# Perceiver layer: which engine normalises the rows of the later context chunks

## The reference

```python
def layer_norm(x, g, b):
    mu = jnp.mean(x, axis=-1, keepdims=True)
    var = jnp.mean((x - mu) ** 2, axis=-1, keepdims=True)
    return (x - mu) * jax.lax.rsqrt(var + EPS) * g + b

xn = layer_norm(x, g1, b1)            # context, (2, 2048, 512)
ln_lat = layer_norm(latents, g2, b2)
q = ln_lat @ Wq
kv = jnp.concatenate([xn, ln_lat], axis=1) @ Wkv
k, v = jnp.split(kv, 2, axis=-1)      # 16 heads of 64
weight = jnp.einsum('bhld,bhnd->bhln', q * scale, k * scale)
weight = softmax(where(full_mask, weight, neg))
out = jnp.einsum('bhln,bhnd->bhld', weight, v) @ Wout
```

## Time and profile before

| | us |
|---|---|
| median of 3 runs | 868.83 (868.0 to 869.57) |
| profiled execution | 869.66 |
| its span, first to last instruction | 867.9 |
| PE busy | 840.7 (97%) |
| DVE busy | 576.1 (66%) |
| ACT busy | 441.0 (51%) |
| POOL busy | 349.9 (40%) |

### The profile page before, as it was taken

One profiled execution on the slowest core, in us unless ns is written; L12 is line 12 of the kernel. 1 busy time (PEld: TensorE's weight loads), 2 busy tenths in 40 slices (PEclk: granted clock), 3 DMA queues, 4 the chain that ended last, 5 costly groups with the idle time before them and its releaser, 6 DMA issues.

```text
span 867.9 us, 17399 instructions
## 1 busy us (share of the span) xinstructions
PE 840.7 (97%) x6329; PEld 782.9 (90%) x6329; DVE 576.1 (66%) x1536; ACT 441.0 (51%) x1029; POOL 349.9 (40%) x361
## 2 busy tenths in 40 slices
PE   5999999999999999999999999999999999998998
PEld 3999999999999999999999999998977689986886
DVE  7454647566576878656576665777777547766886
ACT  5665454554556464644645545455435434344553
POOL 5742634534463655746454344313301310003443
PEclk9999999999999999999999999999999999999999
DMA  6554427576467757576675664787577676842310
GB/s 215 183 176 164 151 104 238 192 233 226 176 224 256 255 207 280 203 232 201 223 242 205 235 207 163 264 342 256 195 250 298 292 303 273 358 141 102 98 50 25
DMA packets 71126, 183.04 MB, mean 211 GB/s; under 512 B 6353, under 2 KB 19585, under 8 KB 65025
## 3 DMA queue, kind: packets, MB, share of 16 engines
q1 hardware_dynamic: 70944, 181.90, 59.0%
q10 hardware_dynamic: 96, 0.02, 0.0%
HBM read 130.00 MB, written 50.86 MB: 208 GB/s over the span
## 4 chain that ended last, share of the span: by engine, by line
PE 85%; DVE 7%; DMA 4%; issue 2%; ACT 2%; SPq 0%; POOL 0%; DVEq 0%; ACTq 0%
PE pJ L1660 15%; PE pJ L1661 14%; PE pJ L1662 14%; PE pV L1806 7%; PE pS L1784 4%; PE pT L1792 3%; PE pS L1792 3%; PE pS L1660 2%; PE pT L1784 2%; PE pS L1662 2%; PE pS L1661 2%; DMA w_split<-wvst 2%; PE pX L1696 1%; PE pV L1660 1%; PE pV L1661 1%
## 5 line engine op out<-in xcount | busy, mean ns | idle before, releaser
L1660 PE MATMUL pJ<-WV,XT 128*128 128x256 f32 x544 | 158.5, 291 | 0.0
L1661 PE MATMUL pJ<-WV,XT 128*128 128x256 f32 x544 | 153.8, 283 | 0.0
L1662 PE MATMUL pJ<-WV,XT 128*128 128x256 f32 x544 | 153.7, 283 | 0.0
L862 ACT ACTIVATE SP<-SP,xneg 128x768 f32<-128x768 f32 (+1 forms) x96 | 85.8, 895 | 119.3 <-DVE xneg L1235 119.3
L1660 PE MATMUL pJ<-XT,WK 128*128 128x384 f32 (+1 forms) x384 | 126.9, 330 | 3.6 <-DVE XT L1135 1.4
L1662 PE MATMUL pJ<-XT,WK 128*128 128x384 f32 (+1 forms) x384 | 125.2, 326 | 0.0
L1661 PE MATMUL pJ<-XT,WK 128*128 128x384 f32 (+1 forms) x384 | 125.1, 326 | 0.0
L1135 DVE TENSOR_TENSOR KT<-pJ,KT 128x384 fp32r<-128x384 f32 x96 | 51.2, 535 | 89.8 <-ACT KT L839 89.3
L1660 PEld LDWEIGHTS pJ<-WV,XT 128*128 128x128 f32 x544 | 104.1, 191 | 0.2 <-issue 0.2
L1661 PEld LDWEIGHTS pJ<-WV,XT 128*128 128x128 f32 x544 | 104.2, 192 | 0.0
L1662 PEld LDWEIGHTS pJ<-WV,XT 128*128 128x128 f32 x544 | 104.0, 191 | 0.0
(11 more groups left out here) (397 smaller groups left out, 2153.8 us busy)
## 6 DMA issues: line engine op xcount, KB each, us to landing
WS<-w_split SPq DMA_DIRECT2D x14, 2048.0 KB, 8.8
WV<-wv_split SPq DMA_DIRECT2D x20, 1024.0 KB, 7.2
WK<-wk_split SPq DMA_DIRECT2D x40, 512.0 KB, 4.5
w_split<-wkst SPq DMA_DIRECT2D x40, 512.0 KB, 3.6
w_split<-wvst SPq DMA_DIRECT2D x40, 512.0 KB, 3.9
XA<-w_split SPq DMA_DIRECT2D x4, 2048.0 KB, 13.0
xraw<-in_ctx SPq DMA_DIRECT2D x7, 768.0 KB, 6.4
wk_split<-WK SPq DMA_DIRECT2D x8, 512.0 KB, 4.0
```

The lines of the kernel that those rows point to most:

```text
L862: ac.activation(SP[:, I % 2, h, 0:w], SP[:, I % 2, h, 0:w], ACT.Exp, bias=xneg[:, I % 2, h:h + 1], scale=XSC, accum_out=total).then_inc(c_ ...
L1660: te.matmul(dst, a(HI), b(HI), start=start, stop=False)
L1661: te.matmul(dst, a(HI), b(LO), start=False, stop=False)
L1662: return te.matmul(dst, a(LO), b(HI), start=False, stop=stop)
```

## The change

For chunks 3 to 11 (nine chunks, 24 tiles) the rows are normalised by ScalarE. GpSimd computes `nmr = -mean * rstd` behind `rstd` with two small instructions, and ScalarE then applies `rstd * x + nmr` to each tile in place. These instructions stand in ScalarE's list in iterations 3, 7, ... 35, behind the exponentials and `rescale` of the next iteration and ahead of the copy of `V{G}.2`.

```diff
+            def negative_means(C):
+
+                m = ctx_count(C)
+                pool.wait_ge(c_rstd, C + 1)
+                pool.wait_ge(c_norm, C - 2)
+                gp.tensor_tensor(nmr[:, 0:m], mv[:, 0:m, 0], rstd[:, 0:m], ALU.mult).then_inc(s_rst, 1)
+                rs_count[0] += 1
+                pool.wait_ge(s_rst, rs_count[0])
+                gp.tensor_scalar(nmr[:, 0:m], nmr[:, 0:m], -1.0, None, ALU.mult).then_inc(s_nmr, 1)
+
             for I in range(ITERS):
                 step = steps_of(I)
-                C8, C9 = (I + 9) // 4 if (I + 9) % 4 == 0 else 0, (I + 10) // 4 if (I + 10) % 4 == 0 else 0
+                C9 = (I + 10) // 4 if (I + 10) % 4 == 0 else 0
                 if I + 3 < PAIRS:
                     wk_lo(I + 3)
-                if 3 <= C8 < CHUNKS:
-                    normal(1)
-                if 3 <= C8 < CHUNKS:
-                    for t in range(2, ctx_count(C8)):
-                        normal(t)
-                    pool.engine_nop().then_inc(c_norm, 1)
                 if step:
...
                 if 3 <= C9 < CHUNKS:
                     rsqrt(rstd, mv, 3, c_stat, C9 + 1, c_rstd)
-                    pool.wait_ge(c_rstd, C9 + 1)
-                    normal(0)
+                    negative_means(C9)
...
-                pool.wait_ge(s_rst, 1 + CHUNKS + 2 * i + b + 1)
+                pool.wait_ge(s_rst, rs_count[0] + 2 * i + b + 1)
...
                     exps(n, 0)
                     exps(n, 1)
                     rescale(n)
+                C8 = (I + 9) // 4 if (I + 9) % 4 == 0 else 0
+                if 3 <= C8 < CHUNKS:
+                    act.wait_ge(s_nmr, C8 - 1)
+                    for t in range(ctx_count(C8)):
+                        last = ac.activation(xraw[:, t, :], xraw[:, t, :], ACT.Identity, bias=nmr[:, t:t + 1], scale=rstd[:, t:t + 1])
+                    last.then_inc(c_norm, 1)
                 if I % 2 and G < GROUPS:
                     value_hi(G, 2)
```

## The result

The changed kernel takes 885.18 us (median of 4, 882.88 to 886.67) against 868.41 us (867.49 to 869.57) of the kernel before: ratio 1.018, 95% interval 1.016 to 1.020. It is slower by 16.8 us, where 12.3 us were forecast; 885.18 lies within the range, near its upper end. The profiled execution took 882.88 us, with a span of 881.1 us; 882.0 us was worked out for it. The profiled execution is thus met to 0.9 us, and the median is 2.3 us above it. Both parts need an explanation.

A forecast was written before the change was run, and what follows sets the result against it. TensorE, busy 840.7 of 867.9 us, was taken as the bound. Stalls of 12.26 us plus 0.7 for restarts minus a 0.62 gain made 12.3 us, on the median of 868.83 giving 881.1 us; range 875.5 to 885.5.

The forecast's parts named there:

- The bound: TensorE, busy 840.7 of 867.9 us: GpSimd savings are worth nothing by themselves, main-loop waits of TensorE cost their full length.
- The place: In front of `K.1` in iterations 3, 7, ... 35: nine stalls behind the late copy of `V.2`, 12.26 us together.
- The price of an activation: On ScalarE, 0.71 us from start to start: 2.13 us for three tiles, 1.42 for two.
- the bounds on both sides: For one ScalarE activation: 0.52 us at least (forecast 876.5 us), 0.81 us at most (883.5 us).
- The restarts: First TensorE matmul after a wait takes 0.1 us more; at seven places new, 0.7 us in all.
- The wait for `nmr`: ScalarE's wait for GpSimd's two small instructions before the activations, put at nothing.
- The gain of 0.62 us: TensorE's wait for the scales at 308.93, behind VectorE's `join`, should go once GpSimd no longer normalises: 0.62 us.
- The step that failed: Once `K.1` is late, nothing gives the stalls back; ScalarE and VectorE move along with TensorE. Stalls total 12.26 us.
- the start of ScalarE's free time: Start of the `V.2` copy less the idle time before it, for example 150.44 in iteration 7; used for `K.1` stalls.
- The clock: Rival: each of nine stalls lowers TensorE's clock, nine times 1.7 us on top, 896 us; chance 3%.
- the dearer activation: Upper bound for a ScalarE activation, 0.81 us with no overlap: 2.4 us more, 883.5 us.
- single wait of 2.0 us: A TensorE wait in a stretch at full clock that did not lower it; the nine stalls were said to look like it.

The follow-up runs named there:

- split run: The changed kernel with VectorE's negate, one instruction on 128x2, written as two on 128x1: 883.74 us, ratio 1.0159 to the kernel before.
- repeated run: The changed kernel itself, nothing altered, measured again with five executions against 21 of the kernel before: 885.05 us, ratio 1.0188.

## Why the prediction came out as it did

**The bound.** Right: GpSimd was worth nothing (relieved alone, 1.0005), and each wait of TensorE in the main loop was lost for good. What TensorE had lost it never made up within the loop, but for iteration 20 and for some 0.6 us in iteration 40, where the wait behind the small DMA was shorter than in the trace of before.

**The place.** Right. The stall is in front of `K.1`, released by VectorE's low part of `V.2`, nine times, 11.0 us in all where 10 to 12 were forecast. The activations alone give a loss as large as the change's (1.0178), the same ones elsewhere 1.0009, and one of them at each place 1.0039, so that it is the room of each place that counts.

**The price of an activation.** Right: 0.80 us long, 0.71 from start to start; the bounds on both sides were not needed. The restarts, 0.1 us at seven places, are right as well: 0.11 us at each of the seven.

**The wait for `nmr`.** Right at nothing; the two instructions take 0.19 and 0.26 us.

**The gain of 0.62 us.** It came, and was 0.81 us, 0.2 more. The reason was only half right: it was put down to GpSimd's relief, and it comes as much when GpSimd is relieved and TensorE hardly late (0.78 us) as when TensorE is merely late and GpSimd is not relieved (0.80 us).

**The step that failed** is "Nothing gives these stalls back ... ScalarE and VectorE, which follow it, move along", together with the start of ScalarE's free time, taken over from the trace of before for each place. GpSimd does not move along: part of its list is released by DMAs and part had stood behind the normalising, so that its instructions meet other instructions of VectorE than before. Twice they met the negate in front of the exponentials, and ScalarE was free some 0.9 us later than assumed. Iteration 3 came to 3.10 instead of 2.13 us, iterations 14 and 15 together to 1.89 instead of 1.30. The third place is ahead of iteration 23, where the second half of VectorE's `join`, 0.29 us long in the trace of before, stood beside a two-input instruction of GpSimd:

```profile
349.28 1.30 DVE L1290 TENSOR_TENSOR OS<-OF,Omv 64x128 f32<-64x128 f32 x1
...
349.16 1.27 POOL L630 TENSOR_TENSOR wkst<-wkst 128x512 fp32r<-128x512 f32 x1
```

The first half had lasted 0.91 us in the trace of before and takes 0.27 here, so the pair is longer by 0.38 us; with a negate of 0.30 us behind it ScalarE was free 0.43 us later than assumed, and iteration 23 came to 1.88 instead of 1.49. Together the three places are 1.95 us over the forecast. The split run took the first two away in its trace. The third was not tested by itself: in the traces of the repeated and of the split run the `join` is as in before, but starts 0.24 and 0.33 us later against TensorE, and iteration 23 steps back by 1.75 us; why it starts later is not shown.

**The clock.** As a rival it was priced at nine times 1.7 us with 3%; the sum left it out, and the range had 2 us above the dearer activation for it and for restarts. It was neither nine times nor never. The stretch behind iteration 19 came in three of four profiles with all the stalls; over the executions of the repeated run the change loses 1.8 us (by medians) to 2.3 us (by means) more to the clock than the kernel before. The comparison with the single wait of 2.0 us in the earlier trace rows held for seven stalls and not for iteration 19. That iteration has a second wait close ahead, one from the kernel before, but iteration 3 has one too in two of the traces, and the clock stayed full there; so what makes the difference is not shown.

**The account, and the luck in it.** In the profiled execution the difference is 13.2 us, 0.9 over the forecast, and this nearness is partly luck. The three collisions add 1.95 us. Against them stand 0.2 us more gained in iteration 20, 0.35 us in all from the other stalls, and 0.4 us from small steps after iteration 35. The clock took 1.58 us behind iteration 19 and gave back 1.53 at 680, where the stretch of the earlier trace rows did not occur. If the clock's 1.8 us by medians is added to the 13.2, it makes 15.0 us, and beside 21 executions of before 14.9 were measured. The 16.8 us of the first comparison are 1.9 more; the kernel before had a median of 868.41 us in its four executions there and of 869.79 and 870.19 us in the larger sets, so most of these 1.9 us are the spread of the kernel before itself. This is bookkeeping on single traces and not a measurement of each part. By the range, too, it was close: 885.18 is 0.3 us under its upper end.

## What to carry to other kernels

Before adding work to an engine that empties accumulator banks, list for each place when the engine is free and how long the next bank can wait for its copy: an activation of 0.7 us cost 0 to 0.7 us by that room alone, and the same 17 us of work, a few instructions further down the list, cost 1 us instead of 15. Work taken off an engine that nobody waits for is worth nothing, and it shifts that engine's other work onto new neighbours. A long stall can cost more than its length through the clock, 1.6 us more here, but which one does was not to be foreseen from these traces. And the engines that a stalled engine does not hold back move against the others: what they will stand beside then has to be looked up anew.

## What the runs showed of the hardware

An instruction of VectorE on 128x2, 0.17 us long, lasted up to 1.19 us beside a two-input instruction of GpSimd that was already running (in the trace of the change), and up to 0.61 us beside a `CAST` (in the repeated run), and ended 0.02 to 0.03 us behind it. Beside GpSimd's `tensor_scalar` with mean and `rstd` per row (L664, 2.09 us) nine of ten took their usual 0.17 us in the trace of before. Written as two on 128x1 it was not held once in 96 cases. Three of the four traces with all the stalls have 3.4 us at the lower clock behind the two stalls of iteration 19 (1.2 to 1.6 and 2.4 us, with 2 us of matmuls between them); after the seven shorter single stalls of 0.7 to 2.0 us, each in dense matmuls, the clock stayed full in all four. What decides whether the clock falls behind iteration 19, and behind iteration 3 in one profile of four, stays open.
